# A two-layer adaLN kernel: the last step of FP4's rounding constant moves from VectorE to GpSimd

## What is computed

```python
def fp4_quant_dequant(x):
    xb = x.reshape(shape[:-1] + (shape[-1] // BLOCK, BLOCK))
    scale = jnp.maximum(jnp.max(jnp.abs(xb), axis=-1, keepdims=True) / 6.0, 1e-12)
    xn = xb / scale
    idx = jnp.searchsorted(_MID, jnp.abs(xn))
    return (_GRID[idx] * jnp.sign(xn) * scale).reshape(shape)

h = silu(fp4_linear(x, w_gate)) * fp4_linear(x, w_up)
return fp4_linear(h, w_down)
```

## Time and profile before

| what | value |
|---|---|
| median of 3 runs | 736.52 us (735.71 to 736.78) |
| the profiled execution's own time | 740.21 us |
| its span, first to last instruction | 738.4 us |
| TensorE busy | 647.3 us (88%) |
| VectorE busy | 511.4 us (69%) |
| ScalarE busy | 319.5 us (43%) |
| GpSimd busy | 222.5 us (30%) |
| granted clock of TensorE, mean | 0.948 of full |

### The profile page before, as it was taken

How to read it: one execution, slowest core, us unless ns; L and a number is a source line. 1 busy time by engine, 2 the same in 40 slices (tenths; PEclk the granted TensorE clock), 3 DMA queues, 4 the chain that set the end, 5 groups by cost and what they waited for, 6 DMA issues and landing times.

```text
span 738.4 us, 11039 instructions
## 1 busy us (share of the span) xinstructions
PE 647.3 (88%) x3816; PEld 504.9 (68%) x3828; DVE 511.4 (69%) x1465; ACT 319.5 (43%) x644; POOL 222.5 (30%) x225
## 2 busy tenths in 40 slices
PE   5889799988777999988889989958889998799997
PEld 4456687877556778775678777846677786576674
DVE  5957598696768667726669777596865754876665
ACT  1133344445234454543344444523445453554453
POOL 3333654343545211004455435253421102000000
PEclk9989999999879999999999999978999999999999
DMA  8400000000000000000000000000000000000001
GB/s 262 110 0 1 2 1 1 1 0 1 1 0 1 1 1 1 1 1 1 1 1 1 1 1 2 1 1 0 1 1 1 1 1 1 0 16 29 14 19 40
DMA packets 12078, 9.64 MB, mean 13 GB/s; under 512 B 1708, under 2 KB 10744, under 8 KB 12024
## 3 DMA queue, kind: packets, MB, share of 16 engines
q1 hardware_dynamic: 12024, 8.94, 4.1%
HBM read 6.84 MB, written 2.10 MB: 12 GB/s over the span
## 4 chain that ended last, share of the span: by engine, by line
PE 69%; DVE 18%; ACT 5%; POOL 4%; issue 4%; DMA 1%; SPq 0%; ACTq 0%; POOLq 0%
PE ps L777 14%; PE ps L647 12%; PE ps L755 8%; PE ps L606 5%; DVE xn L1320 5%; PE ps L922 4%; PE ps L924 4%; PE ps L923 4%; PE ps L800 3%; PE ps L665 2%; PE ps L801 2%; PE ps L595 2%; PE ps L816 2%; DVE row_max L1357 1%; PE ps L601 1%
## 5 line engine op out<-in xcount | busy, mean ns | idle before, releaser
L1083 ACT ACTIVATE probsT<-ps 128x512 f32<-128x512 f32 (+3 forms) x160 | 85.2, 533 | 180.4 <-PE ps L755 180.4
L777 PE MATMUL ps<-v_sb,probsT 128*128 128x129 f32 (+1 forms) x1148 | 157.1, 280 | 3.7 <-ACT probsT L1085 3.7
L777 PEld LDWEIGHTS ps<-v_sb,probsT 128*128 128x128 f32 (+1 forms) x1148 | 141.5, 191 | 10.6 <-ACT probsT L1085 5.5
L1357 DVE TENSOR_REDUCE row_max<-ps 128x1 f32<-128x512 f32 (+2 forms) x144 | 87.6, 619 | 48.3 <-PE ps L647 18.1
L755 PE MATMUL ps<-ident,probs 128*128 128x128 f32 (+1 forms) x574 | 95.7, 285 | 16.7 <-ACT probsT L1083 6.0
L755 PEld LDWEIGHTS ps<-ident,probs 128*128 128x128 f32 (+1 forms) x574 | 67.5, 143 | 49.0 <-issue 45.3
L1057 ACT ACTIVATE probs<-ps,neg_max 128x512 f32<-128x512 f32 (+7 forms) x158 | 92.8, 618 | 16.9 <-DVE neg_max L1364 16.0
L473 POOL TENSOR_TENSOR rstd<-veps,half 128x4 f32<-128x4 f32 x34 | 34.2, 1012 | 154.1 <-DVE veps L1211 153.9
L501 POOL TENSOR_TENSOR hq<-ha,hp 128x352 f32<-128x352 f32 x32 | 29.9, 934 | 139.5 <-DVE hp L1398 139.5
L647 PE MATMUL ps<-k_high,q_high 128*128 128x512 f32 (+4 forms) x112 | 46.0, 411 | 0.6 <-ACT probs L1005 0.6
L1152 ACT ACTIVATE probs<-ps 128x512 f32<-128x512 f32 x40 | 24.0, 599 | 44.7 <-PE ps L924 44.7
(11 more groups left out here) (240 smaller groups left out, 1380.8 us busy)
## 6 DMA issues: line engine op xcount, KB each, us to landing
out<-x_sb SPq DMA_DIRECT2D x8, 256.0 KB, 2.3
x_sb<-in_L_attn_x SPq DMA_DIRECT2D x2, 512.0 KB, 5.3
hT_all<-in_L_wmod SPq DMA_DIRECT2D x2, 384.0 KB
rope_cos<-table_cos SPq DMA_DIRECT2D x1, 768.0 KB, 7.5
rope_sin<-table_sin SPq DMA_DIRECT2D x1, 768.0 KB, 9.1
rope_cos<-table_cos SPq DMA_DIRECT2D x1, 256.0 KB, 4.1
rope_sin<-table_sin SPq DMA_DIRECT2D x1, 256.0 KB, 5.1
moe_raw<-in_L_ffn_expert_gate_w SPq DMA_DIRECT2D x1, 256.0 KB, 4.2
```

What stands on the lines that cost most here:

```text
L777: mm = pe.matmul(bank(OUT_AT, 0, V_W), probsT[0:size, n % 4, k * P:(k + 1) * P], v_sb[0:size, j, :], start=(c == 0 and k == 0), stop=(c == ...
L1083: ins = act.activation(probsT[:, n % 4, 0:full], bank(TURN, 0, full), ACT.Copy)
L1357: ins = dve.tensor_reduce(dst, ps[:, start:start + width], AX.X, ALU.max, negate=single)
```

## The change

The maximum with 1 and the product with `ROUND`, one `tensor_scalar` on m, leaves VectorE's `quantise`, which now ends with the exponent bits. GpSimd does the same `tensor_scalar` ahead of its own three passes, on hp in `hq_scaled` and on qp in `xq_scaled`, with a wait on its own step semaphore behind it; the counts of that semaphore go from two to three a tile or group. VectorE has 20 links fewer in a batch. The same step on the weights, done once at the start, stays on VectorE.

```diff
--- before.py
+++ after.py
@@ -154,7 +154,7 @@
 ROPE_SUMS = 2 * (GROUPS - 1)
 NORM_GROUPS = (2 * GROUPS, GROUPS, GROUPS)
 parts_before, MAX_PARTS = before(lambda l, i: len(score_chunks(l, i)) if len(score_chunks(l, i)) > 1 else 0)
-STEPS_PER_BATCH = 185
+STEPS_PER_BATCH = 165
 
 
 def build(nc, x, cos, sin, wq, wk, wv, w_gate, w_up, w_down, c0, wmod0, qk, ov, gate_w, lb_bias,
@@ -498,10 +498,12 @@
                     pool.wait_ge(hq_grid, b * TILES + n + 1)
                     if n >= 2:
                         pool.wait_ge(turned, b * IN_TURN + TURN_AT["hq", n - 2] + 1)
+                    pool.tensor_scalar(hp[:], hp[:], 1.0, ROUND, ALU.max, ALU.mult).then_inc(hq_step, 1)
+                    pool.wait_ge(hq_step, b * 3 * TILES + 3 * n + 1)
                     pool.tensor_tensor(hq[:, n % 2, :], ha[:], hp[:], ALU.add).then_inc(hq_step, 1)
-                    pool.wait_ge(hq_step, b * 2 * TILES + 2 * n + 1)
+                    pool.wait_ge(hq_step, b * 3 * TILES + 3 * n + 2)
                     pool.tensor_tensor(hq[:, n % 2, :], hq[:, n % 2, :], hp[:], ALU.subtract).then_inc(hq_step, 1)
-                    pool.wait_ge(hq_step, b * 2 * TILES + 2 * n + 2)
+                    pool.wait_ge(hq_step, b * 3 * TILES + 3 * n + 3)
                     blocks = hq[:, n % 2, :].rearrange("p (k e) -> p k e", e=BLOCK)
                     pool.tensor_tensor(blocks, blocks, qh[:, 2, :].unsqueeze(2).to_broadcast(
                         [P, INNER // BLOCK, BLOCK]), ALU.mult).then_inc(hq_ready, 1)
@@ -510,10 +512,12 @@
                     pool.wait_ge(xq_grid, b * GROUPS + g + 1)
                     if g >= 1:
                         pool.wait_ge(turned, b * IN_TURN + TURN_AT["fp4_in", g - 1] + 1)
+                    pool.tensor_scalar(qp[:], qp[:], 1.0, ROUND, ALU.max, ALU.mult).then_inc(xq_step, 1)
+                    pool.wait_ge(xq_step, b * 3 * GROUPS + 3 * g + 1)
                     pool.tensor_tensor(xq[:], qa[:], qp[:], ALU.add).then_inc(xq_step, 1)
-                    pool.wait_ge(xq_step, b * 2 * GROUPS + 2 * g + 1)
+                    pool.wait_ge(xq_step, b * 3 * GROUPS + 3 * g + 2)
                     pool.tensor_tensor(xq[:], xq[:], qp[:], ALU.subtract).then_inc(xq_step, 1)
-                    pool.wait_ge(xq_step, b * 2 * GROUPS + 2 * g + 2)
+                    pool.wait_ge(xq_step, b * 3 * GROUPS + 3 * g + 3)
                     blocks = xq[:].rearrange("p (k e) -> p k e", e=BLOCK)
                     pool.tensor_tensor(blocks, blocks, qs[:, 2, :].unsqueeze(2).to_broadcast(
                         [P, GROUP * P // BLOCK, BLOCK]), ALU.mult).then_inc(xq_ready, 1)
@@ -1393,10 +1397,7 @@
                     link(dve.scalar_tensor_tensor(
                         out=by_block(a), in0=by_block(src), scalar=TIES_DOWN,
                         in1=scales[:, 1, :].unsqueeze(2).to_broadcast([P, n_blocks, BLOCK]), op0=ALU.mult, op1=ALU.mult))
-                    link(dve.tensor_scalar(m.bitcast(I32), a.bitcast(I32), EXPONENT, None,
-                                           ALU.bitwise_and))
-                    last = dve.tensor_scalar(m, m, 1.0, ROUND, ALU.max, ALU.mult)
-                    return last
+                    return dve.tensor_scalar(m.bitcast(I32), a.bitcast(I32), EXPONENT, None, ALU.bitwise_and)
 
                 def fp4_input(g):
                     def scales_used():
```

## The result

The kernel after takes 752.22 us (median of 4 runs, 751.67 to 753.57), the kernel before 736.65 us in runs beside it. The ratio is 1.0208 with a 95% interval of 1.0177 to 1.0238: 15.6 us slower, where 1.8 us slower was forecast and 741.0 us was the end of the range. The profiled execution took 753.57 us with a span of 751.8 us, 13.4 us more than the earlier trace rows; the 15.6 us are the difference of the medians, and the execution profiled before was 3.6 us slower than its median. What is read from the two profiles has to be held against the 13.4.

A forecast was written before the change was run, and what follows sets the result against it. The chain was 69% TensorE and 18% VectorE, so neither VectorE nor GpSimd was the bound as a whole. Terms of +0.9 us per batch, +1.8 us in all, took the 736.5 us median to 738.3 us, range 734.3 to 741.0.

The forecast's parts named there:

- the price of the new pass: GpSimd's added TENSOR_SCALAR with two operations: taken as 0.80 us on 512 columns and 0.60 us on 352.
- both bounds: Limits for GpSimd's new pass on 512 columns: 0.52 us from a MEMSET, 1.28 us from a two-input TENSOR_TENSOR.
- Slot 4: x only, TensorE standing still for xq: GpSimd starts 0.46 us earlier, needs 0.88 us more, so +0.42 us per batch.
- Slots 8 and 16: h then x on VectorE: its passes wait for GpSimd's, both savings are eaten, +0.7 us at each slot.
- The third rival: VectorE slips between GpSimd passes, slots 8 and 16 cost 0.04 us each: -0.9 us, 735.6 us; chance 0.15.
- Slots 18 to 20: VectorE is the path; two dropped passes give 0.76 us, with less waiting a gain of 0.95 us per batch.
- So it still fits, by little: Slot 19's rstd behind the longer hq chain: first half ends at 230.3 us, VectorE wants it at 230.45.
- The sum: All places together: 0.42 + 0.7 + 0.7 - 0.95 = +0.9 us per batch, +1.8 us in all.
- the first: Less idle time before slot 20 keeps TensorE's clock whole: -1.5 us, 735.0 us; chance 0.24.
- The second: GpSimd's new pass costs as much as one with two inputs: +4.4 us, 740.9 us; chance 0.19.
- the cover of slot 12: In slot 12 TensorE finds xq ready, so the longer GpSimd chain there was costed at nothing.
- L1391 of slot 8 stretches: VectorE's L1391 of x in slot 8 runs into GpSimd's pass and takes about 0.9 us instead of 0.21.

The follow-up runs named there:

- e14: Kernel before with x's step on GpSimd in slot 4 alone and useless TensorE products ahead of its xq waits: 735.07 us, ratio 0.9959.
- e4: Kernel before with x's step moved to GpSimd in slot 12 alone, one place per batch: 740.39 us, ratio 1.0021.
- e9: Kernel before with h's step on GpSimd for twelve tiles per batch, all but slots 8, 16, 18 and 19: 738.63 us, ratio 0.9990.
- e6: Kernel before with 7, 6 and 9 useless TensorE products ahead of its xq waits in slots 6, 10 and 18: 730.75 us, ratio 0.9907.
- e13: Kernel before with useless TensorE products ahead of its xq waits, run again as base for three others on one chip: 732.57 us, ratio 0.9912.
- e8: Kernel before with x's sum, the first of GpSimd's three passes on x, moved to VectorE: 733.31 us, ratio 0.9932.
- e3: Kernel before with x's step moved to GpSimd in slot 4 alone, one place per batch: 737.88 us, ratio 0.9988.

## Why the prediction was wrong

**The step that failed** is the price of the new pass, "I take 0.80 and 0.60 us", and with it both bounds, "The ends are therefore 0.52 and 1.28 us". It measured 1.92 and 1.39 us. The upper end assumed that an instruction with one input can't be dearer than one with two; no row said so. The Trainium skill's figure beside it, 769 ns for a good loop over 512 elements (GPSIMD Engine Reference, 3.1), is not this instruction's either: the measured 1.92 us decides.

**Slot 4**: the steps were right. With the measured price they give 1.92 + 0.08 - 0.46 = 1.54 us; it is 1.5 us at slot 6 in the profile, and 3.5 us for two places in e14.

**Slots 8 and 16**: the mechanism was right, L1391 of x does run into GpSimd's chain and both savings are eaten. My layout with the measured prices gives 1.9 us; 7.1 - 4.8 = 2.3 us were measured. TensorE's delay grows by 2.5 us at slot 10, from 2.8 to 5.3, and by as much at slot 18. The rest is what I had not allowed for: beside VectorE's passes GpSimd's L508 took 1.12 us instead of 0.79, and its last pass on x (L522) 1.22 instead of 1.06. The third rival, that VectorE slips through, fell.

**Slots 18 to 20**: the sign was wrong. I wrote "So it still fits, by little" of rstd, and of slot 19's scales that they wait at the upper price; at 1.39 us both are late, 0.76 us at L1395 and 0.71 us at L1324. TensorE stands still for 2.62 instead of 1.80 us. VectorE had gained some 0.3 us by then, which it loses again with 0.5 us more: the delay goes from 7.4 to 7.9 us, 0.5 us lost per batch in place of 0.95 gained.

**The sum** of what the waits add is 1.5 + 2.5 + 2.5 + 0.5 = 7.0 us per batch, 14.0 in all, beside the 13.4 between the two profiles. On the clock I had put no price outside the rival. In these two profiles its parts nearly cancel, 1.3 + 0.8 - 1.2 - 0.7 = 0.2 us in batch 0, so that the direct steps alone give the size; that is luck of this pair, since executions of the kernel before differ by up to 10 us with the clock. The 2.2 us from 13.4 to the medians' 15.6 lie in where the two profiled executions stand: 3.6 us above the median before, 1.3 us above it after.

**The rivals**: the first (the clock gives back) had no test, because the idle time at slot 20 grew instead of shrinking; the half clock there stayed (a mean of 0.58 from 240 to 244 us, where the earlier trace rows have 0.59 from 235 to 239). It gave back 0.7 us all the same, by falling partly into a wait, and the longer waits ahead of slots 6 and 10, whose clock I had left without a price, took 2.1 us. The second, a dear pass, is what happened, dearer than I allowed.

**Right** were the cover of slot 12 (e4's profile) and of twelve h tiles (e9), that L1391 of slot 8 stretches (to 0.68 us, 0.9 was forecast), and that little of VectorE's saving would reach the path.

## What to carry to other kernels

An instruction that the trace doesn't show on an engine has no upper bound in the rows of another form; measure it alone on that engine in an idle stretch before it goes on a path. Ask of the engine that gets the work whether its result is waited for: the same pass cost 0 in slot 12 and 1.5 us in slot 4. Where TensorE must stand still for another engine, products into a free bank ahead of the wait were worth 0.9% here (e6, e13); the best shift of vector work alone was worth 0.7% (e8), which the intervals don't tell apart. Note the mean granted clock of every execution: without it e3 read as free.

## What the runs showed of the hardware

- GpSimd's TENSOR_SCALAR in f32: 1.92 us on 128x512 and 1.39 us on 128x352 with two operations, 1.49 and 1.09 us with one; a copy of 128x512 took 0.61 us, a TENSOR_TENSOR 1.27 us.
- VectorE's and GpSimd's passes hold each other up: a VectorE pass of 0.43 us took 0.90 us beside one of GpSimd, and a GpSimd pass of 0.79 us took 1.12 us beside one of VectorE.
- Executions of one kernel differ in how long TensorE is at half clock, and in time with it: the kernel before took 732.7 us at mean granted clocks of 0.964 and 0.969, and 741.7 us at 0.950.
